# Selective scan layer: the inputs of all four batches in one pipelined block, the skip term kept in DRAM and added by PE, and 64 steps without a meeting of the engines

## The chip, the cores and the metric

The kernel runs on one core of a Trainium2 chip. The metric is the device time of one execution in microseconds (us). The core's engines run their own instruction queues and wait for each other through semaphores: PE (matrix products into PSUM, with its weight loads shown as PEld), DVE (vector work), ACT (functions of one input), POOL (a second, slower vector engine) and SP (which issues DMAs). On-chip memory is SBUF, with 128 partitions, and PSUM, with 8 banks of 512 fp32 columns per partition.

## The reference

Six layers follow each other: a gated delta net, an attention with a mask, a gated MLP with ternary weights, this selective scan, a full attention and a layer of experts. The change is in the fourth. For 4 batches of 512 tokens with 256 channels it computes, with 512 inner channels (DI) and 16 states (N):

```python
u = _ln(x, ln1_g, ln1_b)
xz = u @ W_in + b_in
xp, z = jnp.split(xz, 2, axis=-1)
yc = causal depthwise convolution of xp over 4 tokens
xc = jax.nn.silu(yc + conv_b)
dbc = xc @ W_xp
dtr, Bs, Cs = jnp.split(dbc, [DT_RANK, DT_RANK + N], axis=-1)
dt = jax.nn.softplus(dtr @ W_dt + b_dt)
dA = jnp.exp(dt[..., None] * A)
dBx = (dt * xc)[..., None] * Bs[:, :, None, :]
# over tokens: h = dA_t * h + dBx_t ; y = einsum('bdn,bn->bd', h, C_t)
y = (y + xc * D_skip) * jax.nn.silu(z)
x = x + y @ W_out + b_out
```

What follows in that layer (a second layernorm and the "waves") is the same in both kernels.

## The kernel before

Channels lie on partitions: the 512 inner channels are CC = 4 groups (index m) of 128, and tokens (T = 512) run along the free dimension. One batch is one turn of a loop of the hardware, `Fori(0, B)` with B = 4, which each engine runs for itself. A turn has three parts.

First the inputs. PE projects four groups of x and four of z (L2635) into the PSUM banks y_ps. ACT copies x out with its bias (L2478), DVE convolves it in four passes (L2566, L2568), ACT takes the silu (L2482, L2485) and the silu of z, the gate (L2489). PE projects xc to rank, B and C rows (L2640); ACT copies them twice (L2492, L2493), DVE splits the rows in a rounded part and a rest (L2576, L2577), and multiplies xc by the skip weight into hC (L2581), which PE later adds to y as if it were a state's product. PE projects the rank rows to the step size (L2646). Its softplus is made as max(v, 0) + ln(1 + exp(-|v|)) with a correction: ACT takes Abs, Exp and Ln (L2500, L2501, L2503), DVE 1 + e, two corrections and the sum (L2585 to L2592), then dtx = dt * xc (L2594). Each function set of ACT has to be loaded before it is used (ACT_TABLE_LOAD).

Then 16 steps, one for each state n. PE spreads the state's row of B and of C over the partitions with a product against a selection matrix that ACT picks (L2509 picks, L2654 spreads). ACT copies B and C from PSUM to SBUF (L2516, L2523) and makes the decay dA in PSUM, one group at a time, two deep (L2528). POOL makes dBx for all groups (L2450), DVE runs four scans (L2605) and multiplies groups 1 to 3 by C (L2611), POOL group 0 (L2457), and PE adds the four products up in y_ps through an identity matrix (L2658, called the sum below). DVE's loop over steps takes two per turn. Inside these loops the value that a semaphore is waited for lies in a register, so that waits bring register instructions with them.

At the end of a batch DVE multiplies y by the gate (L2615), PE projects out (L2698) into the dA banks, DVE adds the result to the residual xa (L2620), and the engines meet: each drains, raises `meet` and waits for the others (`sequence_end`, L2432). Nothing of the next batch starts before. The whole stage starts with a bias add of POOL over all batches (L2440), for which DVE waits before its first convolution.

An engine works through its instructions in the order of the code, so the order of the functions called in each engine's block sets the order of work. Of every buffer that is two deep (dBx, Bs, Cs, picked, hC, dA), the writer waits for the reader of two uses ago.

Of the kernel before, what the change touches and what calls it, by code (L numbers as in the profile page):

```python
# [14 lines left out]
ALU = mybir.AluOpType  # L15
# [8 lines left out]
P = 128  # L24
# [2305 lines left out]
def scan_channels(nc, c, xa, ln, norms_loaded):  # L2330


# [4 lines left out]
    with Scope(nc, "scan") as s:  # L2337
# [7 lines left out]
        neg_a = s.sb("neg_a", [P, CC, NS])  # L2345
        skip = s.sb("skip", [P, CC])
        wout = s.sb("wout", [P, CC, D])
        b_out = s.sb("bout", [P, D])
        pick = s.sb("pick", [LOW + DBC, NS, 2, P])
        loaded = s.sem("loaded")  # L2350

# [15 lines left out]
        xp = s.sb("xp", [P, 2, T])  # L2367
        conv = s.sb("conv", [P, 2, T])
        xc = s.sb("xc", [P, CC, T])
        zs = s.sb("zs", [P, CC, T])  # L2370
        whole = s.sb("whole", [LOW + DBC, T], F32R)
        parts = s.sb("parts", [LOW + DBC, T], F32R)
        low_rank = s.sb("low_rank", [RANK, T])
        v = s.sb("v", [P, CC, T])
        dt = s.sb("dt", [P, CC, T])
        dtx = s.sb("dtx", [P, CC, T])
# [3 lines left out]
        e1 = s.sb("e1", [P, CC, T])[:]  # L2380
        dBx = s.sb("dBx", [P, 2, CC, T])
        h = s.sb("h", [P, CC, T])
        hC = s.sb("hC", [P, 2, CC, T])
        e2, gated = dBx[:, 0], dBx[:, 1]
# [5 lines left out]
        ready0 = s.sem("ready0")  # L2390
        proj_ready = s.sem("proj_ready")
        xp_ready = s.sem("xp_ready")
        conv_ready = s.sem("conv_ready")
        xc_ready = s.sem("xc_ready")
        z_ready = s.sem("z_ready")
        dbc_ready = s.sem("dbc_ready")
        whole_ready = s.sem("whole_ready")
        parts_ready = s.sem("parts_ready")
        rank_ready = s.sem("rank_ready")
        step_ready = s.sem("step_ready")  # L2400
        v_ready = s.sem("v_ready")
        w_ready = s.sem("w_ready")
        log_ready = s.sem("log_ready")
        exp_ready = s.sem("exp_ready")
        dt_ready = s.sem("dt_ready")
        dtx_ready = s.sem("dtx_ready")
        skip_ready = s.sem("skip_ready")
# [3 lines left out]
        B_ready = s.sem("B_ready")  # L2411
        dA_ready = s.sem("dA_ready")
# [4 lines left out]
        Cs_ready = s.sem("Cs_ready")  # L2417
        summed = s.sem("summed")
        gated_ready = s.sem("gated_ready")
        out_ready = s.sem("out_ready")  # L2420
        added = s.sem("added")
        vec = s.sem("vec")
        act_a = s.sem("act_a")
        meet = s.sem("meet")
        passed = s.sem("passed")
        block = s.block()
        LOADS = 12 * 16
        WORKERS = 4
        START = 1
        FREE = 2  # L2430

        def sequence_end(eng, b):  # L2432
            eng.drain().then_inc(meet, 1)
            eng.wait_ge(meet, b * WORKERS + WORKERS)
            eng.sem_inc(passed, 1)

        @block.gpsimd
        def _(pool):
            pool.wait_ge(loaded, LOADS)
            nc.gpsimd.tensor_tensor(xa[:], xa[:], b_out[:].unsqueeze(1).broadcast_to([P, NT, D]), ALU.add  # L2440
                                    ).then_inc(ready0, 1)
            with pool.Fori(0, B) as b:

                pool.wait_ge(dtx_ready, b + 1)
                pool.sem_inc(passed, 1)
                def inputs(n):
                    k = n % 2
                    pool.wait_ge(B_ready, b * NS + (n + 1 + START))
                    pool.wait_ge(scanned, b * (NS * CC) + (n + FREE - 1) * CC)
                    nc.gpsimd.tensor_tensor(dBx[:, k], dtx[:], Bs[:, k, :].unsqueeze(1).broadcast_to([P, CC, T]), ALU.mult).then_inc(dBx_ready, 1)  # L2450
# [10 lines left out]
                for n in range(NS):  # L2461
                    first_group(n)
                    if n + 2 < NS:
                        inputs(n + 2)
# [911 lines left out]
```

## Time and profile before

| | us |
|---|---|
| median of 3 runs | 5562.75 (5556.14 to 5563.07) |
| the profiled execution | 5562.39 |
| its span, first to last instruction | 5560.5 |
| mean granted TensorE clock | 0.954 |
| PE, DVE, ACT, POOL busy in the span | 4891.6, 2998.5, 2205.7, 1063.4 |
| this stage, first input matmul to last output add | 3382.64 to 4073.43 |
| DVE scans (L2605), 256 of them | 292.6 busy, 1204 ns each |
| POOL dBx (L2450), 64 | 289.3 busy, 4522 ns each |

Times are taken in one execution. An engine's busy time is the sum of its instructions; waits, register and branch instructions aren't counted. Rows of a timeline give the start, the duration, the engine and the line, what is written and read, a count where like instructions follow each other (the duration is then that of all), and in brackets how long the engine was idle before and what ended that. PEclk 1.00 is 2.4 GHz, 0.50 is 1.2 GHz. A PE matmul in fp32 shows as two passes, so that x8 is four matmuls.

### The profile page before, as it was taken

How to read it: one execution, taken by the hardware profiler on the slowest of the kernel's cores; microseconds unless marked ns; L12 is line 12 of the kernel's file. 1: busy time of each engine (PE TensorE's matmuls, PEld its weight loads, DVE VectorE, ACT ScalarE, POOL GpSimd, SP SyncE). 2: the span in 40 equal slices, each digit the busy share in tenths (PEclk: the TensorE clock that was granted, in tenths of full speed). 3: DMA queues.
4: the chain of work that ended last, by engine and by line, in shares of the span. 5: the costliest groups of instructions: out<-in, count | busy, mean ns of one | idle time of the engine just before them, and what ended most of it. 6: DMA issues, size and time to landing. Idle time of an engine off the chain costs nothing. (4 is left out here: it accounts for less than half of the span.)

```text
span 5560.5 us, 89468 instructions
## 1 busy us (share of the span) xinstructions
PE 4891.6 (88%) x37194; PEld 2794.0 (50%) x37194; DVE 2998.5 (54%) x5854; ACT 2205.7 (40%) x3528; POOL 1063.4 (19%) x660
## 2 busy tenths in 40 slices
PE   6979996999999999999899995665637999999897
PEld 3468884666666666666444442232223333333465
DVE  5757773555455555555300006778766666666350
ACT  5734432444444444444211114555522544445421
POOL 0145552111011011000000003456541000000021
PEclk9989998999999999999999997899878999999898
DMA  2221111000000000000200000000001000000123
GB/s 87 103 92 49 49 45 41 9 7 27 7 10 18 15 7 21 7 10 4 85 0 0 0 0 28 0 0 0 0 5 39 1 13 1 13 1 1 56 80 105
DMA packets 45387, 144.14 MB, mean 26 GB/s; under 512 B 6928, under 2 KB 18768, under 8 KB 38240
## 3 DMA queue, kind: packets, MB, share of 16 engines
q1 hardware_dynamic: 43472, 134.55, 6.8%
q8 instruction: 279, 4.57, 0.3%
q0 software_dynamic: 1536, 4.20, 0.2%
q14 instruction: 100, 0.82, 0.0%
HBM read 102.69 MB, written 36.04 MB: 25 GB/s over the span
## 5 line engine op out<-in xcount | busy, mean ns | idle before, releaser
L1480 DVE CUSTOM_DVE_ANT_0 ma_prob<-ma_ring,ma_mask 128x400 f32<-128x400 f32 (+1 forms) x1024 | 527.4, 571 | 262.7 <-PE ma_ring L1584 262.7
L1932 DVE TENSOR_REDUCE fa_part<-fa_ring 128x1 f32<-128x512 f32 x768 | 486.6, 681 | 222.3 <-PE fa_ring L2053 203.4
L1879 ACT ACTIVATE fa_prob<-fa_ring 128x512 f32<-128x512 f32 (+1 forms) x832 | 441.6, 598 | 406.3 <-PE fa_ring L2053 328.4
L2053 PE MATMUL fa_ring<-fa_K,fa_Q 32*128 32x512 f32 (+1 forms) x2048 | 530.7, 546 | 2.0
L1493 DVE COPY ma_PT<-ma_ring 128x512 f32<-128x512 f32 x512 | 341.8, 688 | 287.3 <-PE ma_ring L1594 287.0
L1594 PE MATMUL ma_ring<-ident,ma_prob 128*128 128x128 f32 (+1 forms) x3328 | 462.1, 280 | 6.7 <-ACT ma_prob L1439 6.7
L2073 PE MATMUL fa_ring<-fa_Qm,fa_K 32*128 32x512 f32 (+1 forms) x1664 | 457.7, 629 | 2.3 <-DVE fa_Qm L1949 2.3
L1608 PE MATMUL ma_pv<-ma_PT,ma_V 128*64 128x256 f32 (+1 forms) x3328 | 457.8, 393 | 0.0
L2267 PE MATMUL ffn_mid<-ffn_hid,ffn_h 128*128 128x512 f32 x1024 | 441.5, 593 | 9.7 <-DVE ffn_hid L2233 6.3
L1406 POOL TENSOR_SCALAR ma_diag<-ident,ma_rtotal 128x128 f32<-128x128 f32 x256 | 149.7, 602 | 1535.5 <-DVE ma_rtotal L1498 1535.5
L1594 PEld LDWEIGHTS ma_ring<-ident,ma_prob 128*128 128x128 f32 (+1 forms) x3328 | 357.0, 141 | 163.6 <-issue 105.1
L1584 PE MATMUL ma_ring<-ma_K,ma_Q 64*128 64x400 f32 (+1 forms) x2048 | 415.5, 524 | 0.0
L1439 ACT ACTIVATE ma_prob<-ma_prob,ma_neg 128x1601 f32<-128x1601 f32 x256 | 414.6, 1620 | 0.0
L1445 ACT ACTIVATE ma_PT<-ma_ring 128x512 f32<-128x512 f32 (+1 forms) x320 | 189.9, 593 | 482.1 <-PE ma_ring L1594 482.1
L2450 POOL TENSOR_TENSOR scan_dBx<-scan_dtx,scan_Bs 128x2048 f32<-128x2048 f32 x64 | 289.3, 4522 | 283.0 <-DVE scan_dtx L2594 222.6
L1608 PEld LDWEIGHTS ma_pv<-ma_PT,ma_V 128*64 128x64 f32 (+1 forms) x3328 | 198.9, 136 | 264.3 <-issue 178.7
L2267 PEld LDWEIGHTS ffn_mid<-ffn_hid,ffn_h 128*128 128x128 f32 x1024 | 193.9, 190 | 257.3 <-issue 247.8
L2605 DVE TENSOR_TENSOR_SCAN scan_h<-scan_dA,scan_dBx 128x512 f32<-128x512 f32 x256 | 292.6, 1204 | 39.6 <-POOL scan_dBx L2450 21.0
L2239 DVE TENSOR_TENSOR ffn_scaled<-ffn_low,ffn_w_s 128x256 f32<-128x256 f32 x16 | 6.8, 424 | 493.1 <-PE ffn_low L2276 493.1
L2658 PE MATMUL scan_y<-scan_hC,ident 128*128 128x512 f32 x544 | 265.0, 633 | 8.0 <-DVE scan_hC L2611 8.0
L2073 PEld LDWEIGHTS fa_ring<-fa_Qm,fa_K 32*128 32x128 f32 (+1 forms) x1664 | 139.6, 179 | 239.3 <-ACT fa_prob L1879 158.1
L1584 PEld LDWEIGHTS ma_ring<-ma_K,ma_Q 64*128 64x128 f32 x2048 | 177.1, 186 | 150.9 <-issue 70.4
(377 smaller groups left out, 7823.4 us busy)
## 6 DMA issues: line engine op xcount, KB each, us to landing
gd_rows<-gp_tile SPq DMA_DIRECT2D x16, 1024.0 KB, 4.2
gd_c_vg<-gd_rows SPq DMA_DIRECT2D x16, 1024.0 KB
moe_w<-in_moe_w SPq DMA_DIRECT2D x16, 1024.0 KB, 7.0
ma_w<-in_ma_w SPq DMA_DIRECT2D x32, 384.0 KB, 3.1
gd_rows<-gp_gate SPq DMA_DIRECT2D x16, 512.0 KB, 5.1
gd_c_qk<-gd_rows SPq DMA_DIRECT2D x16, 512.0 KB
ffn_h<-in_ffn_h SPq DMA_DIRECT2D x2, 4096.0 KB, 22.7
ma_ctxT<-in_ctxT SPq DMA_DIRECT2D x4, 1601.0 KB, 7.0
```

The lines of the kernel that those rows point to most:

```text
L1439: nc.scalar.activation(rows, rows, ACT.Exp, bias=neg[:, t, h:h + 1], scale=SCALE, accum_out=total[:, t, h:h + 1]).then_inc(exp_ready, 1)
L1480: nc.vector.tensor_tensor_reduce(prob[:, u % 2, t, h, k0:k0 + width], bank("S", u, t, n, h)[:, 0:width], mask[:, b % 2, half * 2 + t, k0:k ...
L1493: nc.vector.tensor_copy(PT[0:n, (u * KT + kt) % NPT, :, :], bank("T", u, kt)[0:n, :].rearrange("p (h q) -> p h q", h=2)).then_inc(dve_take ...
L1584: nc.tensor.matmul(bank("S", u, t, n, h)[:, 0:width], Q[rows, q % 2, q0:q0 + P], K[rows, q % 2, k0:k0 + width], start=True, stop=True).the ...
L1594: last = nc.tensor.transpose(bank("T", u, kt)[0:n, h * QH + t * P:h * QH + (t + 1) * P], prob[:, u % 2, t, h, kt * P:kt * P + n], c.ident[:])
L1608: last = nc.tensor.matmul(pv[u % 2][cols, 0:QH], V[0:n, q % 2, kt, cols], PT[0:n, (u * KT + kt) % NPT, h, :], start=(kt == 0), stop=(kt == ...
L1879: nc.scalar.activation(prob[0:n, (u * KT + kt) % PROBS, j, :], bank("scores", u, kt, j)[0:n, :], ACT.Exp, scale=SCALE).then_inc(p_ready, 1)
L1932: ins = nc.vector.tensor_reduce(part[:, u % 2, t, j, n:n + 1], src[:], AX, ALU.max)
L2053: last = nc.tensor.matmul(bank("chunk", u, i)[:, at * w:(at + 1) * w], Q[rows, b % 2, g, tile * P:(tile + 1) * P], K[rows, b % 2, g, k0:k0 ...
L2073: nc.tensor.matmul(bank("scores", u, kt, j)[0:n, :], K[rows, b % 2, g, kt * P:kt * P + n], Qm[rows, u % 2, :], start=True, stop=True).then ...
L2267: last = nc.tensor.matmul(mid[m % 2][:], w[n][:, k, m * P:(m + 1) * P], hid[e][:, k, :], start=(k == 0), stop=(k == MH - 1))
L2605: nc.vector.tensor_tensor_scan(h[:, m, :], dA[m % 2][:], dBx[:, k, m, :], 0.0, ALU.mult, ALU.add).then_inc(scanned, 1)
```

## The change

The stage is now two blocks, `scan_inputs` and `scan_steps`, without hardware loops; every wait is for a constant. The tiles dt, dtx (first xc, then dt * xc) and parts hold all four batches; gate and skip product of each batch go to DRAM.

In `scan_inputs`, slot j handles x group j + 1 and z group j (16 of each); rank, B and C of a batch follow in the slots of the next. After all slots the softplus is made for all batches in eight pieces of two groups (128x1024), with the intermediate values in PSUM (`high`, `low`), and POOL multiplies dtx.

In `scan_steps`, 64 steps g follow each other. Skip products are loaded to zs and added by PE after step 6 of each batch, then zs is loaded with the gates. Gate and output projection of batch b - 1 stand between the steps 0 and 1 of batch b.

```diff
+def scan_inputs(nc, c, xa, ln, norms_loaded, kept, neg_a, wout, pick, dt, dtx, parts):
...
+        @block.tensor
...
+            project_x(0)
+            for j in range(J + CC):
+                b, m = divmod(j, CC)
+                if j + 1 < J:
+                    project_x(j + 1)
+                if j < J:
+                    project_z(j)
+                if b >= 1 and m == 0:
+                    project_dbc(b - 1)
+                if b >= 1 and m == 1:
+                    project_step(b - 1, 0)
+                    project_step(b - 1, 1)
+                if b >= 1 and m == 2:
+                    project_step(b - 1, 2)
+                    project_step(b - 1, 3)
...
+        @block.scalar
...
+            take_x(0)
+            for j in range(J + CC):
+                b, m = divmod(j, CC)
+                if j + 1 < J:
+                    take_x(j + 1)
+                if 1 <= j <= J:
+                    take_conv(j - 1)
+                if j < J:
+                    take_z(j)
+                if b >= 1 and m == 1:
+                    take_dbc(b - 1)
+                if b >= 1 and m == 2:
+                    take_step(b - 1, 0)
+                    take_step(b - 1, 1)
...
+            exponential(0)
+            exponential(1)
+            act.wait_ge(parts_ready, B)
+            for i in range(4):
+                logarithm(i)
+            act.wait_ge(skip_stored, B * SP_DONE)
+            exponential(2)
+            exponential(3)
+            for i in range(4, 8):
+                logarithm(i)
...
+            def one_more(i):
+                dve.wait_ge(exp_ready, i // 2 + 1)
+                nc.vector.tensor_scalar(pair(high, i), pair(e1[i // 2], i), 1.0, None, ALU.add).then_inc(w_ready, 1)
+
+            def softplus(i):
+                b, v = i // 2, pair(dt[:, i // 2], i)
+                dve.wait_ge(w_ready, i + 1)
+                dve.wait_ge(log_ready, i + 1)
+                nc.vector.scalar_tensor_tensor(out=pair(high, i), in0=pair(high, i), scalar=1.0, in1=pair(e1[b], i),
+                                               op0=ALU.subtract, op1=ALU.subtract)
+                chain.link(nc.vector.scalar_tensor_tensor(out=v, in0=v, scalar=0.0, in1=pair(low, i), op0=ALU.max, op1=ALU.add))
+                nc.vector.tensor_tensor(v, v, pair(high, i), ALU.subtract).then_inc(dt_ready, 1)
...
+            one_more(0)
+            one_more(1)
+            for i in range(2 * B):
+                softplus(i)
+                if i + 2 < 2 * B:
+                    one_more(i + 2)
...
+def scan_steps(nc, c, xa, kept, neg_a, wout, pick, dt, dtx, parts):
...
-            with act.Fori(0, B) as b:
...
+            for g in range(G):
+                decay(g, 0)
+                decay(g, 1)
+                if g + 1 < G:
+                    spread_row(g + 1)
+                copy_C(g)
+                decay(g, 2)
+                decay(g, 3)
+                if g + 2 < G:
+                    pick_rows(g + 2)
...
-                sequence_end(dve, b)
+            for g in range(G):
+                b, n = divmod(g, NS)
+                scans(g)
+                if b >= 1 and n == 1:
+                    add_out(b - 1)
+                against_C(g)
+                if b >= 1 and n == 0:
+                    gate(b - 1)
+            gate(B - 1)
+            add_out(B - 1)
...
+            def spread_B(g):
+                pe.wait_ge(pick_ready, g + 1)
+                if g >= 1:
+                    pe.wait_ge(B_ready, g)
+                nc.tensor.matmul(B_ps[:], picked[:, g % 2, 0, :], parts[:, g // NS, :], start=True, stop=True).then_inc(B_spread, 1)
...
+            for g in range(1, G):
+                b, n = divmod(g, NS)
+                spread_C(g)
+                if b >= 1 and n == 1:
+                    spread_B(g + 2)
+                    project_out(b - 1)
+                    pe.wait_ge(added, TB * b)
+                    add_up(g - 1)
+                else:
+                    add_up(g - 1)
+                    if g + 2 < G:
+                        spread_B(g + 2)
+                if n == 6:
+                    add_skip(b)
+            add_up(G - 1)
+            project_out(B - 1)
```

How the order moves on two engines, where a batch ends. On PE before, L2654 spreads a state's row, L2658 sums, L2698 projects out, and the branch of the batch loop (L2630) follows:

```order
L2654 MATMUL scan_C<-scan_parts,scan_picked 128x512
L2658 MATMUL scan_y<-scan_hC,ident 128x512 x4
L2690 REGISTER_ALU
L2658 MATMUL scan_y<-scan_hC,ident 128x512 x4
L2698 MATMUL scan_dA<-scan_wout,scan_dBx 128x256 x16
L2630 REGISTER_ALU
L2630 COMPARE_AND_BRANCH
```

On PE after the change, from the last step of a batch to step 2 of the next (L2813 spreads B, L2820 spreads C, L2826 sums, L2840 projects out; xnT holds hC):

```order
L2820 MATMUL scst_C<-scan_parts,scst_picked 128x512
L2826 MATMUL scst_y<-xnT,ident 128x512 x4
L2813 MATMUL scst_B<-scan_parts,scst_picked 128x512
L2820 MATMUL scst_C<-scan_parts,scst_picked 128x512
L2813 MATMUL scst_B<-scan_parts,scst_picked 128x512
L2840 MATMUL scst_y<-scan_wout,scst_zs 128x256 x16
L2826 MATMUL scst_y<-xnT,ident 128x512 x4
L2820 MATMUL scst_C<-scan_parts,scst_picked 128x512
```

The output projection now stands behind a B spread of the next batch and ahead of the sum of that batch's step 0. On DVE before, the last scans and product of a batch, gate (L2615) and output adds (L2620):

```order
L2604 REGISTER_ALU
L2605 SCALAR_TENSOR_TENSOR scan_h<-scan_dA,scan_dBx 128x512
L2607 REGISTER_ALU
L2610 REGISTER_ALU
L2611 TENSOR_TENSOR scan_hC<-scan_h,scan_C 128x1536
L2595 REGISTER_ALU
L2595 COMPARE_AND_BRANCH
L2613 ISA
L2615 TENSOR_TENSOR scan_dBx<-scan_y,scan_zs 128x512 x4
L2620 ISA
L2620 TENSOR_TENSOR ss_xa<-ss_xa,scan_dA 128x256
```

On DVE after the change, the same place (L2771 scans, L2779 multiplies by C, L2786 gates, L2793 adds out):

```order
L2771 SCALAR_TENSOR_TENSOR scst_h<-scst_dA,scst_dBx 128x512 x4
L2779 TENSOR_TENSOR xnT<-scst_h,scst_C 128x1536
L2786 TENSOR_TENSOR scst_zs<-scst_y,scst_zs 128x512 x4
L2771 SCALAR_TENSOR_TENSOR scst_h<-scst_dA,scst_dBx 128x512 x4
L2793 TENSOR_TENSOR ss_xa<-ss_xa,scst_y 128x256 x4
L2779 TENSOR_TENSOR xnT<-scst_h,scst_C 128x1536
```

Register and branch rows are gone, and the gate and the adds have scans of the next batch around them.

## Rows read from the trace of the kernel before

**Rows 1.** Timeline, inputs of the second batch (start us, duration us, engine, line)
```profile
3562.15 13.99 PE L2635 MATMUL scan_y<-xnT,scan_win 128*128 x32 [1.31 <-DVEq L2433]
...
3582.05 3.69 PE L2646 MATMUL scan_y<-scan_low_rank,scan_wdt 16*128 16x512 f32 x8 [0.68 <-ACT scan_low_rank L2492]
...
3586.50 1.91 ACT L2500 ACTIVATE scan_e<-scan_v 128x2048 f32<-128x2048 f32 x1
```

**Rows 2.** Timeline, softplus and first scan of the second batch
```profile
3589.72 1.91 ACT L2501 ACTIVATE scan_e<-scan_e 128x2048 f32<-128x2048 f32 x1
...
3591.66 1.23 DVE L2585 TENSOR_SCALAR scan_dBx<-scan_e 128x2048 f32<-128x2048 f32 x1 [6.33 <-ACT scan_e L2501]
...
3597.58 2.29 DVE L2592 TENSOR_TENSOR scan_dt<-scan_dt,scan_e 128x2048 f32<-128x2048 f32 x1
...
3599.91 2.29 DVE L2594 TENSOR_TENSOR scan_dtx<-scan_dt,scan_xc 128x2048 f32<-128x2048 f32 x1
...
3602.53 8.96 POOL L2450 TENSOR_TENSOR scan_dBx<-scan_dtx,scan_Bs 128x2048 f32<-128x2048 f32 x2 [60.18 <-DVE scan_dtx L2594]
...
3607.45 4.57 DVE L2605 TENSOR_TENSOR_SCAN scan_h<-scan_dA,scan_dBx 128x512 f32<-128x512 f32 x4 [5.25 <-POOL scan_dBx L2450]
```

**Rows 3.** Timeline, end of the second batch
```profile
3714.75 1.75 DVE L2611 TENSOR_TENSOR scan_hC<-scan_h,scan_C 128x1536 f32<-128x1536 f32 x1
...
3720.30 2.48 DVE L2615 TENSOR_TENSOR scan_dBx<-scan_y,scan_zs 128x512 f32<-128x512 f32 x4 [3.79 <-PE scan_y L2658]
...
3722.84 8.71 PE L2698 MATMUL scan_dA<-scan_wout,scan_dBx 128*128 128x256 f32 x32 [2.58 <-DVE scan_dBx L2615]
...
3731.69 0.42 DVE L2620 TENSOR_TENSOR ss_xa<-ss_xa,scan_dA 128x256 f32 x1 [1.30 <-PE scan_dA L2698]
...
3732.82 13.99 PE L2635 MATMUL scan_y<-xnT,scan_win 128*128 x32 [1.28 <-DVEq L2433]
```

**Rows 4.** Timeline of DVE, two steps of the second batch
```profile
3641.91 4.56 DVE L2605 TENSOR_TENSOR_SCAN scan_h<-scan_dA,scan_dBx 128x512 f32<-128x512 f32 x4 [0.22 <-DVE scan_hC L2611]
...
3646.59 1.75 DVE L2611 TENSOR_TENSOR scan_hC<-scan_h,scan_C 128x1536 f32<-128x1536 f32 x1
...
3648.70 4.57 DVE L2605 TENSOR_TENSOR_SCAN scan_h<-scan_dA,scan_dBx 128x512 f32<-128x512 f32 x4 [0.35 <-DVE scan_hC L2611]
...
3653.55 1.75 DVE L2611 TENSOR_TENSOR scan_hC<-scan_h,scan_C 128x1536 f32<-128x1536 f32 x1 [0.28 <-DVE scan_h L2605]
...
3655.52 4.57 DVE L2605 TENSOR_TENSOR_SCAN scan_h<-scan_dA,scan_dBx 128x512 f32<-128x512 f32 x4 [0.22 <-DVE scan_hC L2611]
```

**Rows 5.** Timeline, first matmuls and first absolute value of the first batch
```profile
3382.64 16.83 PE L2635 MATMUL scan_y<-xnT,scan_win 128*128 x32 [3.99 <-issue]
...
3415.67 1.91 ACT L2500 ACTIVATE scan_e<-scan_v 128x2048 f32<-128x2048 f32 x1
```

**Rows 6.** Timeline of PE and ACT, one step of the second batch
```profile
3642.24 3.60 PE L2658 MATMUL scan_y<-scan_hC,ident 128*128 128x512 f32 x8
...
3643.25 0.69 ACT L2528 ACTIVATE scan_dA<-scan_dt,scan_neg_a 128x512 f32<-128x512 f32 x1
...
3644.99 0.40 ACT L2509 ACTIVATE scan_picked<-scan_pick 112x256 fp32r<-112x256 f32 x1
...
3645.49 0.57 PE L2654 MATMUL scan_B<-scan_parts,scan_picked 112*128 112x512 f32 x1
```

**Rows 7.** Timeline, last output add and start of the next scope
```profile
4073.01 0.42 DVE L2620 TENSOR_TENSOR ss_xa<-ss_xa,scan_dA 128x256 f32 x1 [1.31 <-PE scan_dA L2698]
...
4074.93 8.80 POOL L2734 TENSOR_TENSOR x<-x,ss_xa 128x4096 f32<-128x4096 f32 x1 [20.81 <-DVEq L46]
```

**Rows 8.** Windows over steps (stretch, length, busy us, PEclk, DMA share, GB/s)
```profile
3607.00:3720.00 113.00, 69.31 (x157) 29.81 (x157) 101.22 (x80) 63.51 (x105) 87.45 (x32) 0.94 0.00 0
...
3615.00:3620.00 5.00, 5.00 (x8) 1.90 (x7) 4.88 (x5) 3.59 (x6) 4.24 (x2) 0.50 0.00 2
```

**Rows 9.** Timeline of PE, a sum at the low clock
```profile
3614.86 6.24 PE L2658 MATMUL scan_y<-scan_hC,ident 128*128 128x512 f32 x8
```

More of the change, by code:

```diff
@@ L2337, in scan_channels @@
     with Scope(nc, "scan") as s:
+        kept = [nc.dram_tensor(f"scan_{n}", [B, P, CC, T], F32).ap() for n in ("gates", "skips")]
+        neg_a = s.sb("neg_a", [P, CC, NS])
+        wout = s.sb("wout", [P, CC, D])
+        pick = s.sb("pick", [LOW + DBC, NS, 2, P])
+        dt = s.sb("dt", [P, B, CC, T])
+        dtx = s.sb("dtx", [P, B, CC, T])
+        parts = s.sb("parts", [LOW + DBC, B, T], F32R)
+        scan_inputs(nc, c, xa, ln, norms_loaded, kept, neg_a, wout, pick, dt, dtx, parts)
+        scan_steps(nc, c, xa, kept, neg_a, wout, pick, dt, dtx, parts)
+def scan_inputs(nc, c, xa, ln, norms_loaded, kept, neg_a, wout, pick, dt, dtx, parts):
+    with Scope(nc, "scin") as s:
         win = s.sb("win", [P, DC, 2 * CH])
@@ new lines, in scan_inputs @@
+        J = B * CC
+        SP_DONE = 16
+        made = s.sem("made")
+        x_projected = s.sem("x_projected")
+        z_projected = s.sem("z_projected")
+        xp_ready = s.sem("xp_ready")
+        conv_ready = s.sem("conv_ready")
+        xc_ready = s.sem("xc_ready")
+        z_ready = s.sem("z_ready")
+        z_stored = [s.sem("z_stored0"), s.sem("z_stored1")]
+        dbc_ready = s.sem("dbc_ready")
+        rank_ready = s.sem("rank_ready")
+        whole_ready = s.sem("whole_ready")
@@ new lines, in _ @@
+        @block.gpsimd
+        def _(pool):
+            pool.wait_ge(loaded, LOADS)
+            for b in range(B):
+                pool.wait_ge(skip_ready, b + 1)
+                rows = xa[:, TB * b:TB * b + TB, :]
+                nc.gpsimd.tensor_tensor(rows, rows, b_out[:].unsqueeze(1).broadcast_to([P, TB, D]), ALU.add)
+            pool.wait_ge(dbc_ready, B)
+            for i in range(2 * B):
+                pool.wait_ge(dt_ready, i + 1)
+                x = pair(dtx[:, i // 2], i)
+                nc.gpsimd.tensor_tensor(x, pair(dt[:, i // 2], i), x, ALU.mult)
@@ L2421, in scan_channels, with _ @@
         added = s.sem("added")
[L2422 to L2425, printed above, removed]
         block = s.block()
[L2427 to L2435, printed above, removed]
+        G = B * NS
+        SP_DONE = 16
+        @block.sync
+        def _(sp):
+            for b in range(B):
+                if b >= 1:
+                    sp.wait_ge(out_ready, TB * b)
+                sp.dma_start(zs[:], kept[1][b]).then_inc(skip_loaded, SP_DONE)
+                sp.wait_ge(skip_summed, b + 1)
+                sp.dma_start(zs[:], kept[0][b]).then_inc(z_loaded, SP_DONE)
+            sp.wait_ge(z_loaded, B * SP_DONE)
@@ L2620, in _ @@
-                    nc.vector.tensor_tensor(row, row, dA[t % 2][:, 0:D], ALU.add).then_inc(added, 1)
-                chain.close()
-                sequence_end(dve, b)
+                    i = TB * b + t
+                    dve.wait_ge(out_ready, i + 1)
+                    nc.vector.tensor_tensor(xa[:, i, :], xa[:, i, :], y_ps[t][:, 0:D], ALU.add).then_inc(added, 1)
+            for g in range(G):
+                b, n = divmod(g, NS)
[5 more added lines that the diff above has]
+                    gate(b - 1)
```

494 lines of the change are left out of this document (243 added, 251 removed).

## The prediction, written before the change was run

> **What bounds the kernel now.** The change touches one stage, so I read by window, not by the page's shares. The page's chain of waits stays in the last layer and says nothing of this stage. The timeline shows four batches one after another. I cut the second, 3562.15 to 3732.82, 170.67 us, into four parts:
> - inputs, 3562.15 to 3586.50: 24.35 us. PE has 48 passes there, 13.99 us for 32 and 3.69 for each of two groups of 8; start to start a pass is 0.427, so 20.5 in all [rows 1];
> - softplus and start, 3586.50 to the first scan at 3607.45: 20.95 us with PE almost idle. ACT, DVE and POOL hand 2048-wide tiles to each other [rows 2];
> - 16 steps, 3607.45 to 3716.50: 109.05 us [rows 2, 3]. DVE sets the pace with 4.57 us of scans and 1.75 us of product, 6.32, and small gaps; two steps take 3655.52 - 3641.91 = 13.61 us, 6.8 each [rows 4];
> - the end, 3716.50 to 3732.11: 15.61 us, and 0.71 to the next batch's first matmul [rows 3].
>
> The first batch takes longer: ACT's absolute value starts at 3415.67, 33.0 us after the first matmul at 3382.64, against 24.35 [rows 5]. So the stage, from that matmul to the last add's end at 4073.43 [rows 7], 690.8 us, is 33.0 + 3 x 24.35 = 106.1 of inputs, 4 x 20.95 = 83.8, 4 x 109.05 = 436.2, and 4 x 15.61 + 3 x 0.71 = 64.6; the sum is 690.7.
>
> **Inputs, pipelined.** PE's work stays 4 x 20.5 = 82.0, and it was already 84% of the part. In the new order PE is stalled where the rank copy queues behind z's gate of its slot (1.5 us), where the step projection waits for the copies of its slot (1.6), and for the last convolution's silu (0.3): 3.4 a batch, three times 10.2. After the last z the same handovers stand alone, 4.4. Each is made of ACT's 0.6 to 0.7 us per 128x512 tile and 0.1 to 0.2 us to wake [rows 6]. The low clock at the start costs 16.83 - 13.99 = 2.9 [rows 1, 5]. 82.0 + 10.2 + 4.4 + 2.9 = 99.5, a gain of 6.6, nearly all from the first batch, where DVE's first convolution no longer stands behind POOL's long bias add. Bounds: 89 (no stalls) and 126 (each later batch costs 8.7 more, as the first did). The eight stores of 1 MB lie beside this: the last gates have some 12 us of tail before their buffer is wanted.
>
> **Softplus, in eight pieces of 1024.** DVE binds it. A two-input pass runs at one element a cycle, 2048 in 2.29 us, 512 in 0.62 [rows 2, 3], so 1024 takes 1.22; three and 0.1 of waits are 3.75. The "+1" took 1.23 for 2048 from SBUF to SBUF, two elements a cycle; its output now lies in PSUM, which no row shows. The ends are that rate (0.69 for 1024) and the gate's rate, whose input is in PSUM (1.22); I take 1.22. In order: Abs, table and Exp 5.1; the first softplus at 11.4, behind the second Exp and the table for Ln; then 4.97 a piece, with one stop of near 3 for the exponentials of batches 2 and 3, which ACT starts only after the fourth logarithm; DVE ends at 51.5, POOL's last product, 1024 wide, 2.4 later: 54 (51.8 at the double rate). The change of scope costs 1.5 (last add's end 4073.43, next instruction 4074.93 [rows 7]). The start of the steps, once and not four times, is pick, spread and copy (2.2), POOL's 4.5, and 0.4 to wake: 7.1. So 62.6 for 83.8, a gain of 21.2; bounds 58 and 70.
>
> On the rate into PSUM the Trainium skill ("VectorE: DVE Perf Modes", Why PSUM operands drop a tier) says that fp32 with any PSUM operand runs at one a cycle; by it the time stands as forecast, by the SBUF row it is 2.2 us less. The skill's "ScalarE: Activation LUTs", What ACT_TABLE_LOAD costs, puts a switch at 1283 ns and a drain of 1380 ns. In the trace Exp starts 1.31 us after Abs has ended [rows 1, 2]: the load is there, the drain isn't. By the page's figure three switches on the path would add 4.1 us, 5525.
>
> **64 steps.** DVE's gaps alternate: 0.12 and 0.35 around one product, 0.28 and 0.22 around the next [rows 4]; the 0.35 crosses the loop's branch. In straight code I take 0.32 a step instead of 0.49: 6.64, and 64 x 6.64 = 425, plus 0.7 for the low clock at the start. Bounds: 409.6 (0.04 a gap, as from 3599.87 to 3599.91 [rows 2], where a pass waits only for the one before) and 436.2 (nothing changes). POOL is next, 87.45 us busy in 113 beside DVE's 101.22 [rows 8], and waits for Bs besides; that leaves it about 1 us a step. ACT has 0.25: its third exponential ends at 3643.94, the third scan starts 2.28 after 3641.91, at 3644.19 [rows 4, 6].
>
> **Skip sum, once per batch.** Four more matmuls, 3.6 us [rows 6], in step 6. PE's step is 0.3 + 3.6 + 0.5 = 4.4 and becomes 8.0: the next C spread is 1.4 late, ACT's copy of C too, less the 0.25: 1.1 on the path, four times 4.4. Before, this sum ran while the batch's start waited for DVE.
>
> **Three seams in place of three meetings.** DVE gates a batch (2.48 + 0.1 [rows 3]) between two steps, since its sums are done. Then PE should project out, but ahead of that stands the B spread for two steps on, and it waits for the pick, the last piece of ACT's step: that starts 3.1 us after the scans do, and the spread 0.5 later, lasting 0.6 [rows 4, 6]. So the projection starts 4.3 after the gate, not at once. From its start to the last add's end are 9.27 (3722.84 to 3732.11 [rows 3]); PE has idled over 5 us before it instead of 2.6, so I add 1.0 for a longer low clock (bounds 0, and 6.4: 8.71 x 6.24/3.60 - 8.71, by the sum's time at either clock [rows 6, 9]). DVE finishes the step's scans 4.7 after the gate and waits until 14.6: 9.9. PE then makes up a sum (3.6) before the next C spread, and by ACT's copy the third scan is 1.3 late. A seam is 2.6 + 9.9 + 1.3 = 13.8, three are 41.4. The last end is 15.4. So 425.7 + 4.4 + 41.4 + 15.4 = 486.9 for 436.2 + 64.6 = 500.8, a gain of 13.9.
>
> **Sum.** 99.5 + 62.6 + 486.9 = 649.0 for 690.7, or 41.7 less. The profiled run took 5562.39 (span 5560.5 and 1.9 around it), 0.4 under the median of the runs. 5562.4 - 41.7 = 5521; nothing outside the stage moves.
>
> **Rivals.**
> - The gaps stay. Registers may be handled while DVE computes, and the gaps be the price of four waits: 436.2 - 425 = 11.2 more, 5532. For it: the product after 0.12 has register work ahead of it too. Against: the wide gap is at the branch.
> - The gaps nearly vanish: 15.4 less, 5505. Against: a step has more semaphores than the dependent passes.
> - The slots of the input block miss each other. Its buffers are two deep and ACT has three tiles in a slot of 3.4 us of PE; if each batch then costs what the first did, 3 x 8.7 = 26 more: 5547.
> - Slower: PE stays at the low clock in the steps. It is busy 4.4 of 6.6 us and idles in each. At half the clock the sum takes 6.24 even where the clock rises within it [rows 9]; PE's 4.4 doubled is 8.8 and PE binds: 64 x (8.8 - 6.64) = 138, so 5659. From 20 such steps on the gain is gone. Against: over 16 steps the granted clock was 0.94, 0.50 only near their start [rows 8], with longer idling per step.
> - The change doesn't do what it says: a seam costs what the end and a restart of DVE did, near 28 us, by a longer wait on C's path. Three times 14 more is 5563, no change.
>
> **Chances.** Forecast 0.66 (its own range 5509 to 5533), gaps stay 0.12, gaps vanish 0.10, inputs miss 0.07, seams like meetings 0.02, low clock 0.03. The range 5503 to 5548 leaves out the last two and the edges of the others. A difference within 0.2% (11 us) can't be told from none. Faster by more (under 5551.6) 0.93; within it 0.03; slower 0.04.
>
> **What would show it.** Right: the first Abs near 99 us after the first matmul, the first scan near 162; scans 6.6 apart; at each seam a DVE idle near 10 us ended by the output projection, and PE's own idle before that ended by the pick; one longer step after each step 6. Wrong: a "+1" of 0.69; a projection within 1 us of the gate; steps at 6.8; a granted clock of 0.5 between seams.

## The result, and the profile after

The changed kernel took 5510.83 us (median of 4, 5500.06 to 5518.12) beside 5562.0 for the kernel before; the ratio is 0.9912 (95% interval 0.99 to 0.9923). It is faster, and the forecast of 5521 lay 10 us above it. The profiled execution took 5518.12 us (span 5516.0) where that of before took 5562.39, 44.3 us less. By the trace 2.8 lie ahead of the stage (first matmul at 3379.82, was 3382.64) and 41.8 in it, and 0.3 are lost behind it and around the span. "Predicted" is the prediction's own sum, cut at the same places:

| part of the stage, us | before | predicted | after |
|---|---|---|---|
| inputs, first matmul to absolute value | 106.1 | 99.5 | 122.0 |
| softplus and start, to the first scan | 83.8 | 62.6 | 59.9 |
| 64 steps without extras | 436.2 | 425.7 | 412.2 |
| skip sums | in the softplus | 4.4 | 3.2 |
| three seams | in the line below | 41.4 | 36.2 |
| ends | 64.6 | 15.4 | 15.5 |
| sum | 690.7 | 649.0 | 649.0 |

In this execution the total came out to 0.1 us by errors that cancel: the inputs took 22.5 us more than predicted, and the other parts together 22.4 less. That the two are equal is luck. This was also the slowest of the four executions; by the medians the change gained 51.2 us where 41.7 were forecast. The experiments are about both errors.

**Inputs.** Timeline of PE over one batch's step projections in the changed kernel (L2435 projects x and z, L2464 the step):

```profile
3403.90 3.60 PE L2435 MATMUL scin_high<-xnT,scin_win 128*128 128x512 f32 x8
3408.74 1.98 PE L2464 MATMUL scin_low<-scin_low_rank,scin_wdt 16*128 16x512 f32 x4 [1.25 <-ACT scin_low_rank L2514]
3410.65 5.40 PE L2435 MATMUL scin_high<-xnT,scin_win 128*128 128x512 f32 x8
3417.50 2.56 PE L2464 MATMUL scin_low<-scin_low_rank,scin_wdt 16*128 16x512 f32 x4 [1.45 <-ACT scan_dt L2520]
```

The two waits are there and near their forecast (1.25 and 1.45 us, predicted 1.5 and 1.6). What was not forecast is behind them: eight passes take 5.40 us, and 3.60 ahead of the wait. That is the clock, which the windows of the same kernel show (stretch, length, busy us of PE, PEld, DVE, ACT and POOL, PEclk, DMA share, GB/s) over the whole part and over pieces behind waits:

```profile
3379.80:3501.80 122.00, 110.06 (x192) 41.82 (x192) 54.57 (x89) 47.79 (x76) 9.39 (x4) 0.79 0.17 69
3412.00:3416.00 4.00, 4.00 (x6) 1.35 (x4) 1.24 (x2) 1.29 (x2) 0.00 (x0) 0.59 0.00 0
3420.00:3424.00 4.00, 4.00 (x6) 1.84 (x6) 0.00 (x0) 0.19 (x1) 0.00 (x0) 0.50 0.00 0
```

PE is busy for 110.1 us with its 192 passes, predicted 82.0 and 2.9 for the low clock at the start, and idles 11.9 (predicted 14.6 of stalls). In the four separate parts of before it was busy 92.8 and idle 13.2. So the clock, not the handovers, makes the block slower than the four separate ones.

**Softplus and start.** Timeline of the changed kernel, absolute value, exponential and "+1" of the first pieces, then the last piece and the first scan:

```profile
3501.79 1.90 ACT L2524 ACTIVATE scin_line<-scan_dt 128x2048 f32<-128x2048 f32 x1
3503.71 1.28 ACT L2525 ACT_TABLE_LOAD   x1
3505.00 1.91 ACT L2525 ACTIVATE scin_line<-scin_line 128x2048 f32<-128x2048 f32 x1
...
3507.04 2.35 DVE L2610 TENSOR_SCALAR scin_high<-scin_line 128x1024 f32<-128x1024 f32 x2 [10.03 <-ACT scin_line L2525]
...
3516.84 1.23 DVE L2610 TENSOR_SCALAR scin_high<-scin_zs 128x1024 f32<-128x1024 f32 x1
...
3551.93 2.34 POOL L2642 TENSOR_TENSOR scan_dtx<-scan_dt,scan_dtx 128x1024 f32<-128x1024 f32 x1 [1.29 <-DVE scan_dt L2619]
...
3555.14 0.72 ACT L2726 ACTIVATE scst_picked<-scan_pick 112x256 fp32r<-112x256 f32 x2 [9.39 <-PEq L50]
...
3561.65 3.45 DVE L2771 TENSOR_TENSOR_SCAN scst_h<-scst_dA,scst_dBx 128x512 f32<-128x512 f32 x3 [9.80 <-POOL scst_dBx L2703]
```

The "+1", whose output now lies in PSUM, takes 1.23 us for a piece of 1024 elements (2.35 for two), as long as it took for 2048 from SBUF to SBUF [rows 2]. From the absolute value it is 52.5 us to the end of POOL's last product (predicted 54), 0.9 to the steps' first instruction (1.5) and 6.5 to the scan (7.1).

**Steps and a seam.** Timeline of DVE in the changed kernel around the first seam (L2771 scans, L2779 multiplies by C, L2786 gates, L2793 adds out); of the adds the first and the last are shown:

```profile
3665.17 4.57 DVE L2771 TENSOR_TENSOR_SCAN scst_h<-scst_dA,scst_dBx 128x512 f32<-128x512 f32 x4
3669.77 1.75 DVE L2779 TENSOR_TENSOR xnT<-scst_h,scst_C 128x1536 f32<-128x1536 f32 x1
3671.44 2.48 DVE L2786 TENSOR_TENSOR scst_zs<-scst_y,scst_zs 128x512 f32<-128x512 f32 x4
3673.84 4.55 DVE L2771 TENSOR_TENSOR_SCAN scst_h<-scst_dA,scst_dBx 128x512 f32<-128x512 f32 x4
3681.52 0.42 DVE L2793 TENSOR_TENSOR ss_xa<-ss_xa,scst_y 128x256 f32<-128x256 f32 x1 [3.13 <-PE scst_y L2840]
...
3686.79 0.42 DVE L2793 TENSOR_TENSOR ss_xa<-ss_xa,scst_y 128x256 f32<-128x256 f32 x1 [1.30 <-PE scst_y L2840]
3687.13 1.75 DVE L2779 TENSOR_TENSOR xnT<-scst_h,scst_C 128x1536 f32<-128x1536 f32 x1
3688.96 2.34 DVE L2771 TENSOR_TENSOR_SCAN scst_h<-scst_dA,scst_dBx 128x512 f32<-128x512 f32 x2
3692.45 2.34 DVE L2771 TENSOR_TENSOR_SCAN scst_h<-scst_dA,scst_dBx 128x512 f32<-128x512 f32 x2 [1.15 <-ACT scst_dA L2744]
...
3696.67 4.57 DVE L2771 TENSOR_TENSOR_SCAN scst_h<-scst_dA,scst_dBx 128x512 f32<-128x512 f32 x4
3701.26 1.75 DVE L2779 TENSOR_TENSOR xnT<-scst_h,scst_C 128x1536 f32<-128x1536 f32 x1
3703.11 2.34 DVE L2771 TENSOR_TENSOR_SCAN scst_h<-scst_dA,scst_dBx 128x512 f32<-128x512 f32 x2
```

A step is 3703.11 - 3696.67 = 6.44 us. Its gaps are 0.02 ahead of the product and 0.10 behind it, where [rows 4] had 0.12 and 0.35, 0.28 and 0.22. The seam is 2.4 for the gate (3671.44 to 3673.84), 8.7 from the scans' end at 3678.39 to the product, and 1.15 for the third scan. PE beside it, in the same kernel (the last B spread and the projection):

```profile
3677.28 0.80 PE L2813 MATMUL scst_B<-scan_parts,scst_picked 112*128 112x512 f32 x1 [4.88 <-ACT scst_picked L2726]
3677.87 8.88 PE L2840 MATMUL scst_y<-scan_wout,scst_zs 128*128 128x256 f32 x32
```

As predicted, PE idles until the pick (4.88 us) though the gate has ended at 3673.92; the projection starts 3.95 behind the gate (predicted 4.3).

### The profile page after: what moved, and what is told of

It reads as the page before. It is cut to its first block and busy times, and to the rows that moved or that the text cites. A ratio compares the mean times of both kernels' runs of the same rounds, so it can differ in the third digit from the quotient of the medians.

```text
span 5516.0 us, 87839 instructions
## 1 busy us (share of the span) xinstructions
PE 4904.1 (89%) x37194; PEld 2801.5 (51%) x37194; DVE 2994.9 (54%) x5866; ACT 2192.0 (40%) x3522; POOL 1084.4 (20%) x671
## 5 line engine op out<-in xcount | busy, mean ns | idle before, releaser
L2771 DVE TENSOR_TENSOR_SCAN scst_h<-scst_dA,scst_dBx 128x512 f32<-128x512 f32 x256 | 292.9, 1204 | 21.4 <-POOL scst_dBx L2703 9.8
L2703 POOL TENSOR_TENSOR scst_dBx<-scan_dtx,scst_Bs 128x2048 f32<-128x2048 f32 x64 | 289.5, 4523 | 60.6 <-ACT scst_Bs L2732 60.5
L2826 PE MATMUL scst_y<-xnT,ident 128*128 128x512 f32 x512 | 249.4, 633 | 4.0 <-DVE xnT L2779 2.5
```

The lines of the kernel that those rows point to most:

```text
L2771: nc.vector.tensor_tensor_scan(h[:, m, :], dA[m % 2][:], dBx[:, g % 2, m, :], 0.0, ALU.mult, ALU.add).then_inc(scanned, 1)
```

## The experiments

They were timed in three groups, each beside the kernel before (its medians 5560.34, 5559.58 and 5557.81); a ratio is against that. The four parts of each profiled execution are cut as above: inputs, softplus and start (59.86 to 59.88 in every version of the changed kernel), steps with skip sums and seams, end. None leaves computation out. All but two are versions of the changed kernel. What is not changed varies too: over all traces the stage's first matmul lies between 3377.8 and 3386.5, and from its last add to the end of the span it is 1487.1 to 1491.4 us, so that a single total says less than the parts.

**The changed kernel again**, unaltered.

> The changed kernel once more, unaltered. Its input block took 122.0 us in the first profile (first matmul to first absolute value) against the 99.5 of the prediction, with PE at the low clock in many stretches. Theory A (short stalls of PE drop its clock): the block's length depends on where the stalls fall against the clock's changes, so it varies from run to run, 105 to 125 us, and the time with it, 5500 to 5520. Theory B (a fixed queueing in the slots, clock only a consequence): the block again takes 122 us within 1.

5513.15 us (5511.0 to 5513.67), ratio 0.9914 (0.9898 to 0.9931). Steps 451.56, end 15.47: as in the first trace to 0.1. The inputs took 110.2 us at a clock of 0.87, not 122.0 at 0.79, while PE's idle time was the same 11.9. Each batch but the last has two of the short waits, six in all. In the first trace the granted clock falls to 0.50 behind each of the six, in this one behind three of them; from 3424 to 3460, behind the other three, it stays 1.00. So the input block has no one length: the same program, with the same waits, loses a different amount to the clock.

**The step projections one slot later.**

```diff
-                if b >= 1 and m == 1:
+                if b >= 1 and m == 2:
                     project_step(b - 1, 0)
                     project_step(b - 1, 1)
-                if b >= 1 and m == 2:
+                if b >= 1 and m == 3:
                     project_step(b - 1, 2)
...
```

On ACT take_step 0 and 1 go ahead of z's gate of slot 3, take_step 2 and 3 to the slot behind it.

> In the input block the step projections stand one slot later and ACT copies their results another slot on, so PE no longer waits there (1.25 and 1.45 us in each batch). Theory A (these waits make the clock fall): the block takes 92 to 98 us instead of 122, granted clock near 1 until the tail, time about 5488. Rival (the clock falls by PE's load as such, the waits themselves are all that is lost): 3 batches x 2.7 = 8 us less, block near 114.

5497.67 us (5486.03 to 5499.77), ratio 0.988 (0.9864 to 0.9897). Inputs 92.3 us. The waits of PE over the input block in this version (what waits, for what: us in total, times, longest), and its window:

```profile
PE scin_low L2464 <- ACT scan_dt L2520: 0.7, 2, 0.3
PE scin_low L2464 <- ACT scin_low_rank L2514: 0.7, 1, 0.7
```

```profile
3386.50:3478.70 92.20, 90.24 (x192) 36.03 (x192) 54.50 (x89) 47.80 (x75) 9.39 (x4) 0.94 0.22 92
```

With the waits went 9.9 us of PE's idle time, and with them PE's own time fell from the 98.3 and 110.1 of the changed kernel to 90.2 us for the same 192 passes: the clock came back. Not wholly: behind a wait of 0.34 us that is left, eight passes from 3447.10 on still take 5.40 us. The time missed its forecast of 5488 by 10 us. That was reckoned from a block of 122 us, while the unaltered kernel of the same group had 110.2; the steps took 2.2 us more, and what follows the stage 3.6.

**The waits filled.** Two matmuls whose results nobody uses stand ahead of the step projections that wait.

```diff
             def project_step(b, m):
                 i = CC * b + m
+                if m in (0, 2):
+                    for k in range(2):
+                        nc.tensor.matmul(low[:, 3, :], win[:, k % 2, 0:P], c.xnT[:, k % 2, 0:T], start=True, stop=True)
                 pe.wait_ge(rank_ready, b + 1)
```

> Two matmuls into an unused bank (4 passes, 1.7 us at full clock) stand before each pair of step projections, where PE waits 1.25 to 1.45 us; 16 matmuls more, output unchanged. Theory A (the clock falls through the waits): PE has no wait there, keeps the full clock, and the block takes about 103 to 108 us in spite of the added work. Rival (the waits, not the clock, cost; or the load): 13.7 us of passes less 10 us of covered waits, block 122 to 126.

5503.8 us (5499.12 to 5508.44), ratio 0.9895 (0.9879 to 0.9912). 105.85 us of inputs, but with 224 passes in them. Waits of PE there, and its window:

```profile
PE scin_low L2455 <- ACT scan_dtx L2502: 2.5, 1, 2.5
```

```profile
3381.50:3487.30 105.80, 102.66 (x224) 41.71 (x224) 54.51 (x89) 47.77 (x75) 9.41 (x4) 0.97 0.19 80
```

Only the wait for the last silu is left and the clock is 0.97. The 32 added passes are 13.7 us of work at 0.427 each; without them stands 92.2, the time of the version above. Taking the waits away by reordering and filling them with idle work both bring the clock back. To the kernel the first is worth more: its median is 15.5 us under that of the unaltered kernel of the same group, this one's 9.4.

**The same matmuls behind the projections**, as a control; 28 passes more.

```diff
+                if m in (1, 3) and i < CC * B - 1:
+                    for k in range(2):
+                        nc.tensor.matmul(low[:, 3, :], win[:, k % 2, 0:P], c.xnT[:, k % 2, 0:T], start=True, stop=True)
```

> Control to the filled waits: the changed kernel with the same added matmuls (two of 512 columns, four passes, results not used) behind the step projections of groups 1 and 3 instead of ahead of those of groups 0 and 2, and none at the very last, so 28 passes more than the 192, near 12 us of PE work at full speed. Theory (it is PE's waits in the input block that are followed by the low clock): PE still idles about 12 us there, the granted clock over the inputs stays at 0.79 to 0.90, and the inputs take what the unaltered block took, 107 to 122 us, plus some 8 to 14: 115 to 136. Rival (only how much work PE has counts, wherever it stands): the clock is 0.95 or more and the inputs take near 106, as with the waits filled. A third: the passes push PE's own work behind ACT's, the waits shrink by themselves and the time comes out near 108 with a clock between the two.

5521.51 us (5519.28 to 5523.91), ratio 0.9933 (0.9917 to 0.995). Waits of PE over the input block, and its window:

```profile
PE scin_low L2464 <- ACT scin_low_rank L2517: 4.4, 4, 1.2
PE scin_low L2464 <- ACT scan_dt L2523: 4.3, 3, 1.4
PE scin_low L2455 <- ACT scan_dtx L2502: 2.5, 1, 2.5
```

```profile
3383.20:3508.40 125.20, 113.26 (x220) 44.92 (x220) 54.48 (x89) 47.76 (x76) 9.39 (x4) 0.88 0.16 67
```

Every wait is as long as in the changed kernel, the clock is 0.88, and 125.2 less 12.0 for the passes is 113.2. Nearly the same work in the other place leaves the clock within the 0.79 to 0.90 of the unaltered block. The rival by which only the amount of work counts is out.

**The kernel before with its hardware loops written out** (all six `Fori` of this stage), nothing else; every wait is then for a constant.

```diff
-            with dve.Fori(0, B) as b:
+            for b in range(B):
...
-                with dve.Fori(0, NS // 2) as i:
+                for i in range(NS // 2):
...
```

> The kernel before with every hardware loop of this stage written out (six of them), so that all waits are for constants; meetings, order and softplus stay as they are. Theory A (the gaps between DVE's passes come from loop and register work): steps fall from 6.81 to the 6.44 of the changed kernel, 64 x 0.37 = 24 us less, and a few us more in the inputs. Rival (the gaps come with the meetings or the free count of the semaphores): steps stay at 6.8, gain under 5 us.

5528.46 us (5527.38 to 5536.2), ratio 0.9947 (0.993 to 0.9963). Timeline of DVE, steps of the second batch:

```profile
3624.21 4.57 DVE L2605 TENSOR_TENSOR_SCAN scan_h<-scan_dA,scan_dBx 128x512 f32<-128x512 f32 x4
3628.81 1.75 DVE L2611 TENSOR_TENSOR scan_hC<-scan_h,scan_C 128x1536 f32<-128x1536 f32 x1
3630.69 4.57 DVE L2605 TENSOR_TENSOR_SCAN scan_h<-scan_dA,scan_dBx 128x512 f32<-128x512 f32 x4
```

A step is 6.48 us with gaps of 0.03 and 0.13. 16 steps take 103.7 to 104.3 us (109.1 before), 20.8 less in all, as forecast to 3 us, and the passage to the next batch 0.2 (0.7). The first batch's inputs took 30.2 (33.0), but that isn't the loops: the next version, which keeps the batch loop, has 30.3. Writing the loops out brings 31 of the 47 to 51 us between the two kernels. The four input parts together are 102.9 us, less than the 107 to 122 of the pipelined block.

**Before, DVE's inner loop alone written out**; its waits are still for register values.

```diff
-                with dve.Fori(0, NS // 2) as i:
+                for i in range(NS // 2):
```

> The kernel before with only DVE's inner loop over pairs of steps written out; its waits still use a register, since the loop over batches stays. Theory A1 (the branch makes the gap, as the prediction had it): the 0.35 before every second scan falls to about 0.22, 32 x 0.13 = 4 us less. Theory A2 (registers in the waits make it): within 1 us of before. If the branch made all of the difference to the changed kernel, 24 us less.

5557.57 us (5548.84 to 5564.8, 10 runs), ratio 0.9994 (0.9984 to 1.0003): no difference that can be told, though 4 us less were expected. DVE's timeline, second batch:

```profile
3642.60 1.75 DVE L2611 TENSOR_TENSOR scan_hC<-scan_h,scan_C 128x1536 f32<-128x1536 f32 x1
3644.57 4.57 DVE L2605 TENSOR_TENSOR_SCAN scan_h<-scan_dA,scan_dBx 128x512 f32<-128x512 f32 x4 [0.21 <-DVE scan_hC L2611]
3649.26 1.75 DVE L2611 TENSOR_TENSOR scan_hC<-scan_h,scan_C 128x1536 f32<-128x1536 f32 x1
```

The gaps are 0.12 and 0.22, 6.66 a step. So of the 0.49 us of gaps per step some 0.15 were the branch. From here to the version above, with 0.16, the loops of all engines go and with them the waits for register values: 0.18, most likely the waits. The rest, 0.12 to 0.16, stays in straight code. In the profiled execution the steps are 7.3 us shorter in all, 1.6 of which the four ends give back (64.1 us for 62.5), and what follows the stage takes 3.5 more.

**Seams in series.** Gate, projection and adds follow the last product at once, and the next batch's steps wait.

```diff
-                if b >= 1 and n == 1:
-                    add_out(b - 1)
                 against_C(g)
-                if b >= 1 and n == 0:
-                    gate(b - 1)
+                if n == NS - 1:
+                    gate(b)
+                    add_out(b)
```

On PE the last sum and the projection go ahead of the next batch's spreads.

> The changed kernel, but DVE gates and adds out right after a batch's last product and PE projects out before the next batch's spreads, so that nothing of the next batch lies beside a batch's end. Theory A (a seam costs 12.1 now, and 15.5 for an end alone with 1 to 2 for the restart): seams of 16 to 18 us, 12 to 18 us more in all, steps between unchanged. Rival (the overlap is most of what the change gained): over 25 us more.

5520.08 us (5514.64 to 5526.08), ratio 0.9926 (0.991 to 0.9943). DVE's timeline at the first seam:

```profile
3653.61 1.75 DVE L2779 TENSOR_TENSOR xnT<-scst_h,scst_C 128x1536 f32<-128x1536 f32 x1
3659.15 2.48 DVE L2786 TENSOR_TENSOR scst_zs<-scst_y,scst_zs 128x512 f32<-128x512 f32 x4 [3.79 <-PE scst_y L2823]
3665.41 0.42 DVE L2793 TENSOR_TENSOR ss_xa<-ss_xa,scst_y 128x256 f32<-128x256 f32 x1 [3.77 <-PE scst_y L2837]
...
3670.93 4.56 DVE L2771 TENSOR_TENSOR_SCAN scst_h<-scst_dA,scst_dBx 128x512 f32<-128x512 f32 x4
```

The seams cost 15.5, 15.5 and 13.8 us, and 0.4 to 0.5 each in later steps; those of the changed kernel 12.2, 12.4 and 11.7. The overlap that the change arranges is worth 2.6 to 3.7 us a seam, near 10 in all. The seams came out just under the 16 to 18 us that were expected, and the time, each version taken beside its own runs of before, 8 to 12 us above the unaltered kernel's, where 12 to 18 were expected. Its input block, at 106.8, was a short one. A seam in series costs 14.3 to 15.9 with what comes later, and the end and passage of before, with their meeting, 16.3 (15.6 and 0.7). So the meeting itself cost little; what it kept from overlapping cost more.

**The projection first**, ahead of the B spread that waits for the pick.

```diff
                 if b >= 1 and n == 1:
-                    spread_B(g + 2)
                     project_out(b - 1)
+                    spread_B(g + 2)
```

> In step 1 of batches 1 to 3 PE's output projection stands ahead of the B spread that waits for ACT's pick. Theory A (the pick delays the projection by 4 us and DVE waits for it): projection starts within 0.3 us of the gate's end, a seam costs about 8 us instead of 12.1, 11 us less in all. Rival (the C spread and the sum after it bind): DVE's wait moves from the adds to the third scan, less than 4 us in all.

5500.73 us (5500.02 to 5502.92), ratio 0.9894 (0.9877 to 0.991). PE's timeline at the first seam:

```profile
3660.13 0.77 PE L2820 MATMUL scst_C<-scan_parts,scst_picked 112*128 112x512 f32 x1 [2.31 <-issue]
3662.48 9.29 PE L2840 MATMUL scst_y<-scan_wout,scst_zs 128*128 128x256 f32 x32 [1.58 <-DVE scst_zs L2786]
```

PE now waits 1.58 us for the gate itself. Seams cost 8.7, 8.1 and 8.6 us, the steps 442.7. That is 9 less than unaltered (10.8 at the seams; a second skip sum at 2.0 us instead of 0.4 gives some back), and it shows that the 4 us between gate and projection were the queue on PE, as the prediction had it.

**Three edits together**: step projections one slot later, projection first, and the adds behind the product of step 1 rather than ahead of it.

```diff
                 scans(g)
-                if b >= 1 and n == 1:
-                    add_out(b - 1)
                 against_C(g)
+                if b >= 1 and n == 1:
+                    add_out(b - 1)
```

> Three edits together: step projections one slot later in the input block, the output projection ahead of the B spread, and DVE's output adds after the product of the seam's step instead of before it. By the two runs before, the inputs take 92 us and a seam loses 3.5; moving the adds lets the product lie beside the projection, 1.75 less per seam, unless PE's sum then comes late for the next C (then 0). Expected: inputs 92, seams 6.5 to 8.5, time 5482 to 5488. Rival (the low clock moves into the steps and takes it back): over 5495.

5483.36 us (5476.67 to 5486.88), ratio 0.9859 (0.9843 to 0.9876); inputs 90.6 at a clock of 0.96, steps 441.4. DVE's timeline behind the first seam:

```profile
3664.55 2.34 DVE L2773 TENSOR_TENSOR_SCAN scst_h<-scst_dA,scst_dBx 128x512 f32<-128x512 f32 x2 [2.99 <-ACT scst_dA L2746]
```

The seams cost 8.1 to 9.0, no less than in the version above: the third scan now waits 2.99 for a decay that stands behind ACT's copy of C, and this behind PE's sum. Moving the adds only moved the wait, which is the case for which the expectation had allowed 0.

**And the sums behind the spreads of C.**

```diff
                     project_out(b - 1)
                     spread_B(g + 2)
-                    pe.wait_ge(added, TB * b)
-                    add_up(g - 1)
+                elif b >= 1 and n == 2:
+                    pe.wait_ge(added, TB * b)
+                    add_up(g - 2)
+                    spread_B(g + 2)
+                elif b >= 1 and n == 3:
+                    add_up(g - 2)
+                    spread_B(g + 2)
+                    add_up(g - 1)
```

> The version with all three edits, and PE's two sums after a seam now stand behind the next spreads of C: the sum of step 0 in step 2 and that of step 1 in step 3, each behind that step's spread of C. Theory: in the version before it the third scan of step 2 waits 2.99 us for the decay, which stands behind ACT's copy of C, which waits for PE's spread behind the sum; with the spread first that wait goes and about 1.3 comes back a step later, where two sums stand together. A seam costs about 2.2 for the gate, 2.9 for the adds and 1.3, so 6.4 for 8.1 to 9.0, three times some 2 us: 5 to 7 us less in the steps, the steps near 435 us, the kernel near 5478. Rival: the sum of step 0 now holds up DVE's product of step 2, which needs the buffer, by as much as was won, and the seams stay at 8 to 9: 5483, or even more if the B spread that stands behind the sum is late for POOL.

5476.87 us (5469.3 to 5481.92), ratio 0.9857 (0.9841 to 0.9874). DVE's timeline behind the first seam:

```profile
3661.45 4.57 DVE L2773 TENSOR_TENSOR_SCAN scst_h<-scst_dA,scst_dBx 128x512 f32<-128x512 f32 x4 [0.20 <-DVE xnT L2781]
...
3670.41 2.34 DVE L2773 TENSOR_TENSOR_SCAN scst_h<-scst_dA,scst_dBx 128x512 f32<-128x512 f32 x2 [0.18 <-ACT scst_dA L2746]
```

The 2.99 is gone; 0.3 to 0.4 comes back in step 4, where 1.3 was expected. Seams cost 6.0, 5.7 and 5.9 with what comes back in the next steps, 7.7 less in all where 5 to 7 was expected; the steps take 431.7, 9.7 less than in the version above, since the skip sums were 1.6 cheaper in this execution. Between the medians lie 6.5 us, and the intervals of the two ratios overlap, so that by the runs alone this last edit isn't told from none; the trace shows its gain at each of three seams. Against the changed kernel it is 30 to 34 us less, each taken beside its own runs of before (80.9 for 47.2 and 51.2).

## Why the prediction was right, and where it was not

- **The time** was right to 0.2%, but the likeliest case was not what happened: its input block and its steps both failed, and the sum held because the two missed in opposite directions. That is luck.
- **The input block** failed, 22.5 us too short in the profiled execution and 10.7 in the repeat. The step that failed is the sum "82.0 + 10.2 + 4.4 + 2.9 = 99.5", which counts the stalls and a low clock at the start alone. The stalls were sized well (11.9 for 14.6 with the tail); what they do to the clock was not counted at all. The rival "the slots miss each other" (26 us) was priced above all that was measured (7 to 22.5), and its mechanism was another: the handovers stay short, and PE runs at 0.5 of full speed for stretches behind them. This is shown by the four versions without the waits or with filled ones, at 0.94, 0.96, 0.96 and 0.97, against 0.79, 0.87, 0.90, 0.90 and 0.88 in the five executions with them. The pipelining was forecast to gain 6.6 us here, and lost 1 to 16 to the kernel before (106.0) and 4 to 19 to its straight version (102.9): the unaltered block took 122.0, 110.2, 106.9 and 106.8. With the step projections one slot later it gains 14 to 15 (92.3, 90.6 and 90.9), so pipelining is not what lost.
- **The step** failed the other way, 6.64 for 6.44, 12.8 us over 64 steps, and 0.7 more for a low clock at the start that took nothing here (0 to 0.6 in other versions). The step that failed is "In straight code I take 0.32 a step instead of 0.49"; it is 0.12. I took two thirds of the wide gap for something that stays; in straight code the gaps are those of dependent passes and 0.1. "The gaps nearly vanish" was priced at 409.6 and is what came (412.2); I gave it 0.10. My argument against it was the number of semaphores, but ten waits for constants a step leave 0.12 us.
- **The seams** were right in mechanism, item by item (2.4, 8.7 and 1.15 for 2.6, 9.9 and 1.3). The projection started 3.95 instead of 4.3 behind the gate and took 8.88 instead of the 9.7 I allowed. The 28 us a seam in the rival "a seam costs what the end and a restart of DVE did" are worked out from no row; with nothing beside it a seam cost 14.3 to 15.9.
- **Softplus and start** were right to 2.7 us, and the pass into PSUM took the longer of its two times, 1.23 us for 1024 where the double rate gives 0.69. With what the Trainium skill says ("VectorE: DVE Perf Modes", Why PSUM operands drop a tier) the trace agrees. The table load starts 0.02 us behind the absolute value's end and takes 1.28, and the exponential starts 0.01 behind it: again there is no room for the drain that the prediction cites.
- **Skip sums**: 0.4 us in three batches and 2.0 in one, for 1.1 each. The two values go with the granted clock of step 6. Over the 36 batches in the nine traces of the changed kernel and its versions it is 1.00 in 24, and they lose 0.4; it is 0.74 to 0.76 in 12, and they lose 1.9 to 2.0. At full clock the four matmuls cost less than the 1.1; what sets the clock there wasn't tested. The windows of the changed kernel's step 6, third batch and second:

```profile
3831.80:3838.30 6.50, 6.46 (x13) 3.12 (x14) 6.34 (x6) 4.19 (x7) 5.25 (x2) 0.74 0.00 0
3716.00:3722.50 6.50, 6.50 (x16) 3.12 (x17) 6.38 (x6) 4.21 (x7) 5.83 (x3) 1.00 0.01 3
```
- **The rivals** "low clock in the steps" (clock 0.92 there) and "seams like meetings" did not come; nor did "the gaps stay".

How the 47 to 51 us divide: 31 from written-out loops, which the kernel before could have had alone, and the other 16 to 20 from the new structure, in which the softplus once instead of four times (84 to 60 us) is the large gain and the input block a loss.

## What to carry to other kernels

A short wait of PE inside a dense stretch costs more than its length, because the granted clock may fall behind it. Before pipelining a stretch that already runs at full clock, place each consumer one slot further from its producer, and look at PEclk and the time per pass and not only at idle time. Where one engine's queue sets the pace with passes of a few us, try written-out loops and constant waits first, and alone. At a seam, look in each queue for what stands between two instructions that depend on each other: here one spread ahead of the projection and one sum ahead of a spread were worth 11 and 8 us over three seams, the second on top of the first and with the adds moved.

## What the runs showed of the hardware

- Waits of 1.25 and 1.45 us in a stretch where PE is otherwise busy were followed by stretches at a granted clock of 0.5 (1.2 GHz), eight passes in 5.40 us instead of 3.60, behind six of six such waits in one execution and three of six in another. The same 192 passes kept PE busy 110.1 us in the one, 98.3 in the other and 90.2 without the waits, so this part of a kernel's time varies from run to run.
- The branch of DVE's loop of two steps cost 0.15 us per step. Waits for constants instead of register values, ten of them a step on DVE, went with 0.18 less per step; they weren't changed alone, but together with the loops of all engines.
- Four more matmuls on PE in a step that DVE paces cost the step 0.4 us at a granted clock of 1.00 and 1.9 to 2.0 at 0.74 to 0.76.
- Of three DVE passes of 1024 in a piece, each 1.21 to 1.23 us long, the one that neither reads nor waits for the last result starts 1.14 after it, the one that does both 1.25. The rows are in the changed kernel's softplus:

```profile
3548.25 1.23 DVE L2616 SCALAR_TENSOR_TENSOR scin_high<-scin_high,scin_skipped 128x1024 f32<-128x1024 f32 x1
...
3549.39 1.21 DVE L2618 SCALAR_TENSOR_TENSOR scan_dt<-scan_dt,scin_low 128x1024 f32<-128x1024 f32 x1
3550.64 1.22 DVE L2619 TENSOR_TENSOR scan_dt<-scan_dt,scin_high 128x1024 f32<-128x1024 f32 x1
```
